# Perceiver block, wide cross attention: value projections of the last head group moved behind its scores, keys turned half a projection later, first weights loaded one stage earlier

## What is computed

```
kvx = einsum('bsi,oi->bso', cond, w_kv_x)            # cond: 4096 x 512
kx, vx = split(kvx, 2)                               # 8 groups x 128 columns each
kx = layernorm(kx) * kxln_w + kxln_b                 # over the 128 columns
scores = einsum('bsghd,btgd->bghst', qx, kx) / sqrt(128)
xout = einsum('bghst,btgd->bsghd', softmax(scores), vx)
cat = concatenate([self_attention_output, xout])     # quantised and projected in the next stage
```

## Time and profile before

| | us |
|---|---|
| median of 3 runs | 2843.72 |
| the profiled execution | 2838.31 |
| its span | 2836.5 |
| wide stage, first matmul to last reciprocal's start | 203.65 to 1180.91 |
| TensorE busy, whole span | 2398.9 (85%) |
| VectorE, ScalarE, GpSimd busy | 1769.9, 1223.4, 608.0 |

### The profile page before, as it was taken

The page is one execution under the profiler, slowest core; times in us unless marked ns, Lnnn a source line. Parts: engine busy times, 40 slices in busy tenths (PEclk is TensorE's granted clock), DMA queues, the critical chain, the costliest instruction groups (busy, mean ns, idle before and its releaser), DMA issues. The chain is left out here.

```text
span 2836.5 us, 33142 instructions
## 1 busy us (share of the span) xinstructions
PE 2398.9 (85%) x11416; PEld 1614.4 (57%) x11416; DVE 1769.9 (62%) x3492; ACT 1223.4 (43%) x2116; POOL 608.0 (21%) x505
## 2 busy tenths in 40 slices
PE   3679999999999998567775869788888868899998
PEld 3556666666666665255553426455545425577776
DVE  7744556565565655868887765777777742364444
ACT  4433565666665665322222103566676850111111
POOL 8610133333333334313332002110102000000000
PEclk8889999999999999788887889999999968999999
DMA  3410000000000000133331030000000003276662
GB/s 134 154 72 0 12 6 7 12 1 12 12 1 12 1 4 1 60 124 101 102 99 49 1 145 6 5 5 5 6 5 1 1 19 131 104 273 218 234 223 90
DMA packets 40285, 173.22 MB, mean 61 GB/s; under 512 B 5520, under 2 KB 10512, under 8 KB 29392
## 3 DMA queue, kind: packets, MB, share of 16 engines
q1 hardware_dynamic: 40144, 171.39, 16.7%
HBM read 168.75 MB, written 2.62 MB: 60 GB/s over the span
## 5 line engine op out<-in xcount | busy, mean ns | idle before, releaser
L373 PE MATMUL wide_a<-wide_w,ctxT 128*128 128x256 f32 x2048 | 457.1, 380 | 6.2 <-DMA wide_w<-hbm_wkvx 6.2
L373 PEld LDWEIGHTS wide_a<-wide_w,ctxT 128*128 128x128 f32 x2048 | 385.2, 191 | 59.0 <-issue 9.5
L356 POOL TENSOR_TENSOR wide_sums<-wide_sums,wide_s 128x512 f32<-128x512 f32 x224 | 294.6, 1315 | 480.2 <-ACT wide_s L478 466.7
L508 DVE BATCH_NORM_STATS2 wide_stats<-wide_keys 128x6 f32<-128x128 f32 x256 | 62.3, 285 | 307.5 <-ACT wide_values L463 307.1
L394 PE MATMUL wide_o<-wide_s,wide_values 128*128 128x512 f32 x512 | 236.3, 605 | 14.8 <-ACT wide_s L478 14.7
L1448 ACT ACTIVATE int_prob<-int_a,int_shift,qscale 128x512 uint8<-128x512 f32 x256 | 199.2, 787 | 100.6 <-PE int_a L1340 99.9
L386 PE MATMUL wide_scores<-wide_q,wide_keysT 128*128 128x512 f32 x512 | 237.1, 603 | 5.0 <-ACT wide_s L474 5.0
L474 ACT COPY wide_s<-wide_scores 128x512 f32<-128x512 f32 x256 | 149.2, 586 | 180.0 <-PE wide_scores L386 180.0
L1529 DVE TENSOR_REDUCE int_peaks<-int_a 128x1 f32<-128x512 f32 x256 | 169.2, 685 | 58.8 <-PE int_a L1340 56.7
L1340 PE MATMUL int_a<-int_keys,qrows 96*128 96x512 bf16 x512 | 166.4, 408 | 40.9 <-DVE int_peaks L1529 34.2
L532 DVE TENSOR_TENSOR wide_top<-wide_top,wide_s 128x512 f32<-128x512 f32 x240 | 165.6, 690 | 16.7 <-ACT wide_s L474 10.9
(11 more groups left out here) (383 smaller groups left out, 4336.9 us busy)
## 6 DMA issues: line engine op xcount, KB each, us to landing
moe_gate_up<-hbm_m_gu SPq DMA_DIRECT2D x34, 1408.0 KB, 6.1
moe_down<-hbm_m_down_a SPq DMA_DIRECT2D x34, 512.0 KB, 7.0
causal_wqkv<-hbm_wqkv SPq DMA_DIRECT2D x8, 1536.0 KB, 6.5
causal_raw<-hbm_ffn_units SPq DMA_DIRECT2D x48, 256.0 KB, 2.6
ctxT<-hbm_ctxT SPq DMA_DIRECT2D x4, 2048.0 KB, 13.9
oproj_raw<-hbm_wproj SPq DMA_DIRECT2D x8, 1024.0 KB, 4.9
ctxT_again<-hbm_ctxT SPq DMA_DIRECT2D x4, 2048.0 KB, 17.1
moe_down<-hbm_m_down_b SPq DMA_DIRECT2D x34, 192.0 KB, 7.3
```

Source lines behind the costliest of these rows:

```text
L356: ins = pool.tensor_tensor(sums[0][:, :], before, part[:, j, :], ALU.add)
L373: mm = pe.matmul(a[h][:, j, :], ctxT[:, kc, t * P:(t + 1) * P], w[g % 2][:, kc, :], start=(kc == 0), stop=(kc == KC - 1))
```

## The change

Three edits, all around the wide stage:

1. The first group's weights are loaded by the block that also loads the context, ahead of the context, and so before the self attention. `w` and its semaphores move out of the stage for that. In the stage itself SyncE issues only the loads of groups 1 to 7.
2. `turn(n-1)` now stands behind project(n, 0), where turn(n) stood at the end of step n; `keep_turned(n-1)` stands between keep(n, 0) and keep(n, 1) on ScalarE.
3. In the last group (`LATE = 56`, steps 56 to 63) `project` and `keep` handle the 128 key columns alone. `project_values(m, h)` projects the value columns in step m + 9, just ahead of weigh(m-1); `keep_values` copies them on ScalarE, behind exponential(m-1). Two semaphores, `values` and `values_kept`, order them; `weigh(m)` waits for `values_kept`, and the first `project_values` for the last `keep`.

```diff
+    LATE = N - QPG
-        w = [st.sb(f"w{i}", [P, KC, 2 * D]) for i in range(2)]
-                    sp.dma_start(w[g % 2][:, :, :], wkv_dram[g]).then_inc(s_w[g % 2], 16)
+                    if g >= 1:
+                        sp.dma_start(w[g % 2][:, :, :], wkv_dram[g]).then_inc(s_w[g % 2], 16)
@@ project
+                    cols = slice(0, 2 * D if n < LATE else D)
-                            mm = pe.matmul(a[h][:, j, :], ctxT[:, kc, t * P:(t + 1) * P], w[g % 2][:, kc, :],
+                            mm = pe.matmul(a[h][:, j, cols], ctxT[:, kc, t * P:(t + 1) * P], w[g % 2][:, kc, cols],
+                def project_values(m, h):
+                    g, c = divmod(m, QPG)
+                    pe.wait_ge(s_kv, 2 * N)
+                    if m > LATE:
+                        pe.wait_ge(s_vk, 2 * (m - 1 - LATE) + h + 1)
+                    for j in range(2):
+                        t = 4 * c + 2 * h + j
+                        for kc in range(KC):
+                            mm = pe.matmul(a[h][:, j, D:], ctxT[:, kc, t * P:(t + 1) * P], w[g % 2][:, kc, D:],
+                                           start=(kc == 0), stop=(kc == KC - 1))
+                    mm.then_inc(s_vp, 1)
@@ weigh
+                    if m >= LATE:
+                        pe.wait_ge(s_vk, 2 * (m - LATE) + 2)
@@ TensorE's order
                     if n < N:
                         project(n, 0)
+                    if 1 <= n <= N:
+                        turn(n - 1)
...
                     if n < N:
                         project(n, 1)
+                    if LATE <= n - LAG + 1 < N:
+                        project_values(n - LAG + 1, 0)
+                        project_values(n - LAG + 1, 1)
...
-                    if n < N:
-                        turn(n)
@@ ScalarE
-                    act.copy(values[n % VR][:, 2 * h:2 * h + 2, :], a[h][:, :, D:]).then_inc(s_kv, 1)
+                    if n < LATE:
+                        ins = act.copy(values[n % VR][:, 2 * h:2 * h + 2, :], a[h][:, :, D:])
+                    ins.then_inc(s_kv, 1)
+                def keep_values(m, h):
+                    act.wait_ge(s_vp, 2 * (m - LATE) + h + 1)
+                    if h == 0:
+                        act.wait_ge(s_o, m - VR + 1)
+                    act.copy(values[m % VR][:, 2 * h:2 * h + 2, :], a[h][:, :, D:]).then_inc(s_vk, 1)
@@ ScalarE's order
                         keep(n, 0)
+                    if 1 <= n <= N:
+                        keep_turned(n - 1)
+                    if n < N:
                         keep(n, 1)
...
-                    if n < N:
-                        keep_turned(n)
+                    if LATE <= n - LAG + 1 < N:
+                        keep_values(n - LAG + 1, 0)
+                        keep_values(n - LAG + 1, 1)
@@ the block that loads the context
+                            sp.dma_start(w[0][:, :, :], A["wkvx"][0]).then_inc(s_w[0], 16)
                             for kc in range(KC):
                                 sp.dma_start(ctxT[:, kc, :], A["ctxT"][:, kc, :]).then_inc(s_ctx, 16)
```

More of the change, by code:

```diff
@@ L275, in _, with wide_cross_attention_stage @@
                     assert chain.n == PER, chain.n
-def wide_cross_attention_stage(nc, C, ctxT, s_ctx, wkv_dram, q_dram, vecs, inv_smooth, cat):
+def wide_cross_attention_stage(nc, C, ctxT, s_ctx, w, s_w, wkv_dram, q_dram, vecs, inv_smooth, cat):
     scale = D**-0.5
@@ L320, in wide_cross_attention_stage @@
         f = st.ps("rows", [P, 4, P])
-        s_w = [st.sem(f"w_loaded{i}") for i in range(2)]
         s_ql = st.sem("q_loaded")
         names = ("constants products kept var std normed turned keysT scores s_kept top topT peak rows peak_rows shifted exp summed "
-                 "weighed total half put dve pool")
+                 "weighed total half put values values_kept dve pool")
         (s_c, s_a, s_kv, s_var, s_std, s_kn, s_t, s_kt, s_s, s_se, s_top, s_tt, s_pk, s_row, s_pr, s_sub, s_exp, s_sum,
-         s_o, s_tot, s_half, s_put, s_dve, s_pool) = (st.sem(n) for n in names.split())
+         s_o, s_tot, s_half, s_put, s_vp, s_vk, s_dve, s_pool) = (st.sem(n) for n in names.split())
         with nc.Block() as block:
@@ L461, in keep @@
                             act.wait_ge(s_o, n - VR + 1)
-                    act.copy(keys[n % 2][:, 2 * h:2 * h + 2, :], a[h][:, :, :D])
-                    act.copy(values[n % VR][:, 2 * h:2 * h + 2, :], a[h][:, :, D:]).then_inc(s_kv, 1)
+                    ins = act.copy(keys[n % 2][:, 2 * h:2 * h + 2, :], a[h][:, :, :D])
+                    if n < LATE:
[6 more added lines that the diff above has]
+                    act.copy(values[m % VR][:, 2 * h:2 * h + 2, :], a[h][:, :, D:]).then_inc(s_vk, 1)
                 def root(n):
@@ L2794, in build_fp8_attention @@
                 ctxT = cross.enter_context(nc.sbuf_tensor("ctxT", [P, KC, SC], F32))
+                w = [cross.enter_context(nc.sbuf_tensor(f"wide_w{i}", [P, KC, 2 * D], F32)) for i in range(2)]
+                s_w = [nc.alloc_semaphore(f"wide_w_loaded{i}") for i in range(2)]
                 with Stage(nc, "ctx_load") as st:
@@ L2803, in build_fp8_attention @@
                 self_attention_stage(nc, C, qT, kT, v, inv_smooth, cat)
-            wide_cross_attention_stage(nc, C, ctxT, s_ctx, A["wkvx"], q_dram, vecs, inv_smooth, cat)
+            wide_cross_attention_stage(nc, C, ctxT, s_ctx, w, s_w, A["wkvx"], q_dram, vecs, inv_smooth, cat)
         fp8_output_stage(nc, cat, A["wproj"], wscale, x)
```

## The result

The changed kernel took 2816.7 us (median; 2813.44 to 2819.33, 4 runs), the kernel before 2843.72 (2843.5 to 2843.85); the ratio is 0.9905, with an interval of 0.9887 to 0.9922. The forecast was 2822, range 2811 to 2832. The medians differ by 27.0 us, where the forecast said 21.8. The profiled executions, which the step-by-step sum was made for, took 2838.31 and 2816.3: 22.0 less. Single executions of the kernel before went from 2834.9 to 2846.6 over all timings, so small effects are read from the wide stage alone, whose length varies much less. I measure it from the POOL memset that opens the stage to the last reciprocal's start: 981.06 us before, 959.33 after, 21.7 less. From there to the span's end it is 1655.59 and 1655.73.

A forecast was written before the change was run, and what follows sets the result against it. TensorE was taken as the bound, busy throughout the steady part but with idle time at the start and in the tail. Start -8.8, last group -17, tail +4 made -21.8 us: 2843.7 to 2822, range 2811 to 2832.

The forecast's parts named there:

- Edit 1, the wait: Stage start: TensorE no longer waits for the first weights; 3.45 us less waiting, net gain 3.0.
- The 0.46 charged: Ahead of the self stage: SyncE's one additional DMA issue costs 0 to 0.46 us, charged in full.
- Edit 1, the clock: Stage start: with idle time cut to 2.8 us the clock should not fall; gain 2.3 us, between 0 and 2.34.
- rival B: Stage start: the clock falls all the same, or another wait appears; gain 2.3 less, 2824.5 us; chance 0.14.
- Edit 2 at the start: Stage start: half of step 1's projection fills the wait for step 0's keys; gain 3.45 us.
- Edit 3, the last group: Steps 56 to 63: shorter projections, steps of 11.9 us gated by GpSimd's buffer; 17 us saved, between 12 and 21.
- rival A: Last group: GpSimd's buffers do not gate the short steps, which take 11.0 us; 2812 us in all; chance 0.12.
- rival E: Last group: VectorE's shift slows GpSimd's sum to 9.18 us, steps take 15.6; 2849 us, slower; chance 0.04.
- The 4 us charged for VectorE and GpSimd in each other's way: Last group: VectorE and GpSimd operations meeting in short steps; 4 us taken from a saving of 21.0.
- Edit 3, the tail: After the last transposition: the moved value products make the tail 4.0 us longer, between 0 and 8.
- rival C: Tail: clock falls behind the idle 3.6 us and again at turn_top; tail + 8, 2826 us; chance 0.12.
- The sum: Whole kernel: -8.8 - 17 + 4 = -21.8 us, giving 2822 us; chance 0.50 for 2816 to 2828.

The follow-up runs named there:

- e8: Changed kernel with TensorE also waiting for the second group's weights before its first projection; ratio 0.9933 to the kernel before.
- e3: Edit 3 alone (last group's value products later) on the kernel before; ratio 0.9972.
- e1: Edit 1 alone (first group's weights loaded early) on the kernel before; ratio 0.9977.
- e10: Changed kernel with value products earlier, ten buffers of s, and group 5's division pieces moved from steps 58 to 60 to later places; ratio 0.9901 to the kernel before.
- e12: e10 with the second and third division pieces of group 5 put behind find_peak; 2809.65 us, ratio 0.9889 to the kernel before.
- e2: Edit 2 alone (transposition and its copy later) on the kernel before; ratio 0.9982.
- e5: Changed kernel with ten buffers of s instead of nine; ratio 0.9909 to the kernel before.
- e11: Changed kernel with group 5's division pieces moved out of steps 58 to 60, still nine buffers of s; ratio 0.9927 to the kernel before.
- e6: Changed kernel with value products one step earlier, into the idle time ahead of weighing 54 and turn_top; ratio 0.9891 to the kernel before.
- e4: Changed kernel as it is, timed again beside the kernel before; 2819.83 us against 2842.65, ratio 0.9923.
- e9: Changed kernel with ten buffers of s and group 5's division pieces moved out of steps 58 to 60; ratio 0.9927 to the kernel before.
- e7: Changed kernel with value products one step earlier and ten buffers of s; ratio 0.9885 to the kernel before.

## Why the prediction was right

**Edit 1, the wait.** Expected: start near 200.7, 3.0 gained. The memset at 199.44 is followed by TensorE at 199.78, 0.34 later; before it was 3.8. That is 3.46, less what the extra DMA issue costs. The issue took 0.33 (L2832); whether it shows ahead of the stage can't be read, since the time up to the stage's memset went from 195.37 to 202.03 us over the runs. The 0.46 charged stays open.

**Edit 1, the clock.** Expected 2.3. In the first profile the clock stayed up, and 9.17 us were gained to the first scores, of which the two waits are 3.46 and 3.52: the clock gave 2.2. e8 shows the price from the other side. But the reason given was weak. The wait of 3.71 that "left the next projection at full speed" did so before and in e3, but in e1 it did not. And in e10 and e12 the clock fell though the idle time was 2.77, as in the changed kernel: the first projection's row took 12.28 and 12.29 instead of 10.60, 1.7 lost. So rival B (the clock falls all the same) was not wrong, but something that happens in some executions, 2 of the 10 profiles with a first wait of 2.77 us. The right term would have been 2.3 in most executions and 0.6 in some.

**Edit 2 at the start.** Expected 3.45; e2 alone gains 3.52 there (24.32 to 20.80). Idle ahead of the first transposition is 0.26, as forecast under 0.4. That `keep_turned` would let the exponential start earlier, and that this matters in the last group, is what e3 shows (12.67 against 12.0).

**Edit 3, the last group.** Expected 17, between 12 and 21, with steps of 11.9; measured 18.2, although one transposition more falls into it (18.6 when it is set off), steps of 11.8 to 12.1 and two longer ones. GpSimd's buffer is the gate, as named (e5, e11, rival A out), and its sum took at most 6.11 in these steps, far from rival E's 9.18. The 4 us charged for VectorE and GpSimd in each other's way were too much: `normalise` takes 2.91 beside GpSimd where it takes 1.11 alone (e5 at 1050.72), but in plain steps VectorE had room for that; GpSimd's sum stayed at 5.3 in them, and rose only in the steps with division pieces, to 5.42 and 6.11. Those pieces cost 0.1 and 0.8 beyond 12.0, in TensorE's steps 60 and 61; 1.6 had been charged for them. The longest step is 57, 13.21: `turn_top` waits 0.69 there for the maximum, and with `peak_to_rows` it did not fit into the slack, as had been assumed.

**Edit 3, the tail.** Expected 4.0, measured 6.1; this is the term that was sized wrong, on the way to `turn_top`. The first step that failed is the weighing of step 54: "TensorE idle 3.6, at the edge for the clock", and then costed at full speed. It took 6.52, the clock at 0.50, behind 3.46 idle. With T the last transposition again, it ended at T + 10.4 instead of T + 7.4; 1.0 of these 3.0 only takes the place of the wait for GpSimd that was expected behind it. So `turn_top` came at T + 15.64 instead of T + 13.6, the whole difference; from there to the last reciprocal it is 63.65, predicted 63.6. The second is the wait for GpSimd: its sum beside weighing 54 was taken at the steady 5.31 and took 6.46, so that it gave the buffer back at T + 10.55 and not T + 9.4. e6 shows what that costs where weighing 54 runs at full clock (T is 1075.97 there):

```profile
1080.06 6.46 POOL L356 TENSOR_TENSOR wide_sums<-wide_sums,wide_s 128x512 f32<-128x512 f32 x4 [6.70 <-ACT wide_s L507]
...
1086.67 1.07 ACT L503 COPY wide_s<-wide_scores 128x512 f32<-128x512 f32 x2 [5.49 <-POOLq L360]
```

The first copy comes at T + 10.70 even so, and the last maximum ends at T + 14.74, where T + 13.4 was predicted and the changed kernel has T + 15.52. So with the clock up `turn_top` would have come at about T + 14.9 (an estimate from e6): of the 2.0 us some 1.2 stay for GpSimd's sum, and the low clock adds some 0.8. In e4, e5, e8, e9 and e11 the clock fell at this place too, and never in e6, e7, e10 or e12, where value products fill it. So half of rival C came true each time in these; its second half (`turn_top`) didn't in this kernel, but did in e9, e10 and e11, where `turn_top` waited 2.96 us and more.

**The sum** was right to 0.2 us by luck, because its errors met: the last group 1.6 better (18.6 against 17), the tail 2.1 worse, the 0.46 of the DMA issue not to be seen; the 9.2 at the start (without that issue) were met. It was luck too that the rest of the two profiled executions was alike to 0.3 us, when single executions lie 5 us and more apart. The level, median against profiled execution, was carried over as 5.4; it came out at 0.4, which I put down to the scatter of single executions: in e4, with more executions of the kernel before, the medians differ by 22.8.

## What to carry to other kernels

Work that is moved from a saturated stretch into one with idle time is not free there until it stands exactly in the waits: here 28.6 us moved for 6.1 of tail, and a shift by one step in the order brought that down to 1.8 (e6). Behind the first limit look for the next two: ten buffers released the short steps and gave nothing, until the division pieces were moved as well, and then these had to be put where VectorE waits. An idle time of TensorE like those here, 2.8 to 4.1 us, should be costed at either clock, not at one.

## What the runs showed of the hardware

- The length of TensorE's idle time alone doesn't say whether its clock falls from 2.4 to 1.2 GHz. After 2.77 us idle at the start it fell in two profiles (e10, e12) and not in eight; after 3.71 it fell in one (e1) and not in two (before, e3); after 3.46 or 4.14 ahead of weighing 54 it fell in each of the ten profiles that have this wait; ahead of `turn_top` it fell with waits of 2.96 (e11), 6.22 (e9) and 8.02 (e10). In the changed kernel's tail it was at 0.50 when the weighing had begun; in e10 it fell within the first projection (0.75 in 202:203, from 1.00).
- A fall cost 1.3 to 3.1 us each time (first projections 12.28 and, in e8, 13.66 for 10.60; weighing 54 5.39 to 6.76 for 3.70; `turn_top` to `peak_to_rows` 5.37 in e9 for 4.06).
- Some of VectorE's operations on SBUF tiles are stretched when they meet GpSimd's additions of 1.3 us: L102 takes 0.29 alone (e9, 1084.14) and 1.36 beside one (e5, 1042.58), `normalise` 1.11 and 2.91 for four. Others are not: a pair of `BATCH_NORM_STATS2` took 0.49 in the changed kernel at 1037.62, beside a sum, and in e5 at 1048.72, beside none. GpSimd's own four additions, 5.3 alone, took 6.46 beside weighing 54 in the changed kernel and up to 7.69 in e7. The Trainium skill (SBUF — State Buffer, "Who interferes with whom") says that VectorE in some modes and GpSimd share a pair of ports, which whoever issues first holds for the whole instruction; L102's 1.36 in e5 agrees, beside an addition of 1.27 that had begun 0.06 earlier.
- Executions of one program differ by 5 us either way here, largely in stages outside the change: from the last reciprocal of the wide stage to the span's end it is 1655.73 us in the changed kernel's profile and 1659.48 in e4's, the same program. The wide stage repeated within 0.3 us in these two.
